# Three attention layers in one kernel: Q and K as two float32r halves instead of three bf16 parts, heads in pairs

## The chip, the cores and the metric

One core of one Trainium2 chip runs the whole program in one launch. The metric is the device time in microseconds; each run reports the time of its one core. TensorE (PE) multiplies matrices into PSUM, VectorE (DVE), ScalarE (ACT) and GpSimd (POOL) work on tiles, and SyncE (SP) issues the DMAs. All engines have queues of their own that run in order and are tied together by semaphores.

## The reference, cut to what matters

The input x is 2048 tokens by 256 features, float32. Eight residual blocks follow each other: attention A, a gated feed-forward block, a linear attention with a running sum, the feed-forward block again, attention B, a "hyperbolic" projection, attention C, the projection again. Each starts with a layer norm. All three attentions have 16 heads of 16 features:

```python
# A: causal by multiplication: masked scores are 0 and still count in the softmax
scores = einsum('bthd,bshd->bhts', q, k) * tril
out = softmax(scores / T ** 0.5) @ v
# B: not causal, the difference of two attentions with 8 features a head
score = softmax(attn1 - lam * attn2)        # done as one product over 16 features
# C: causal, one rotary term shared by all heads
scores = (einsum('bhtd,bhsd->bhts', q, k) + einsum('btd,bsd->bts', qr, kr)[:, None]) / sqrt(16 + 64)
```

The weights are scaled so that scores are large. The kernel takes care that they come close to float32 products, and subtracts the true row maximum before the exponential.

## The kernel before, in words

**Parts.** After a projection, VectorE rounds a 128 x 512 tile of Q or K to bf16 (L1165) and takes the remainder (L1166); ScalarE rounds the remainder to bf16 (`middle_part`, L1052), GpSimd takes what is left (`split`, L652), and SyncE writes the three parts to DRAM (`parts_to_dram`, L450). The staging tile `STG` has two buffers; VectorE waits for the DMA of the tile two before. `load_stacks` (L479) reads the parts back as stacks: 16 rows for each of six part products (0·0, 0·1, 0·2, 1·0, 1·1, 2·0), so a head's score is one bf16 matmul over 96 rows. `KROWS` is 99: three more rows carry minus the row maximum in three bf16 parts on the Q side, against rows of ones on the K side. Each group of four heads has its own stack, 12 DMAs of 256 KB, double-buffered by group. The first group's stack comes in four token chunks.

**Two passes.** Scores are computed twice. The first pass has the queries on partitions (`max_piece`, L868), 512 keys a piece, one head after the other; VectorE reduces each bank to a row maximum (L1304; on the diagonal, L1300, with the mask, and in layer C, L1293, with the rope scores added, each by a multiply-and-reduce that waits for the previous one). Per chunk of 512 queries, `neg` (L1315 to L1320) combines the maxima and splits their negative into three bf16 parts, four waits between five operations; TensorE transposes them (`mtr`, L894), VectorE copies the result (L1326), four small DMAs put it into the Q stack (L498). The second pass has the keys on partitions (L916): a unit is one key block of 128 against a chunk of 512 queries, with one score matmul a head, ScalarE's exponential (L1079), and `pv` (L940), four heads on the four 32-column tiles, float32. A unit's `pv` stands two units behind (`LAG`), in the queue ahead of the last two scores of the current unit. Layer A has extra units "e" and "m" for the zero scores beyond the diagonal. In layer C 24 of the 40 units add the rope product on TensorE (`rope_product`, L744, three bf16 matmuls a head); 16 get stored rope scores added by VectorE (L1311).

**Rings and order.** PSUM banks 0 to 3 are four slots for maxima and transposes, 4 to 6 a ring of three for scores, 7 holds the `pv` sum. A score waits for the exponential three scores before it. `Layer.plan` writes the order of steps by hand-set weights: the maxima of the next group (and of later chunks) are spread between the score and `pv` steps of this one, in proportion to their weights. All engines walk the same list. A first list (`L.first`) holds maxima only, the last (`L.last`) has none for a next group. SyncE walks the list too: it issues the maximum rows' DMAs and, in C, the loads of rope scores into a ring of five (L502), after the next group's stack loads.

The ring's wait, as it stands now:

```python
n = L.exp_no[u] + j
if n >= RING2:                                   # RING2 = 3
    pe.wait_ge(L.exp_done, group * L.n_exp + (n - RING2 + 1))
```

## Time and profile before

| | us |
|---|---|
| median of 3 runs (lowest, highest) | 3143.9 (3142.0, 3153.44) |
| span of the profiled execution | 3148.2 |
| TensorE busy | 2717.8 (86%) |
| VectorE busy | 2173.0 (69%) |
| ScalarE busy | 1342.8 (43%) |
| GpSimd busy | 312.2 (10%) |

The page gives no other time for the profiled execution than its span, which runs from the first to the last instruction; so the span is its own time here. The page's clock row stands at 9 or 8 tenths in most slices and at 5 to 8 where a layer begins. Layer A's main stage lies at 153 to 718 us, B's at 1267 to 2048, C's at 2345 to 3071; before each there is a stage of maxima only and a stage of projections, and between A and B the feed-forward and linear blocks (750 to 1150 us). Busy time is what an engine's instructions cover; a matmul's duration is modelled and longer than the distance between starts, so starts are what to read on TensorE.

### The profile page before, as it was taken

What the parts mean: (1) busy time and instruction counts of PE and PEld (TensorE: products, weight loads), DVE (VectorE), ACT (ScalarE), POOL (GpSimd) and SP (SyncE); (2) the same over time, 40 slices, a digit from 0 to 9 for tenths busy, and PEclk for the clock granted to TensorE, in tenths of its full rate; (3) what the DMA queues carried; (4) which work ended last, traced back from release to release, by engine and by line L of the source; (5) the groups of instructions that cost most, each with busy time, mean ns of one, the idle gap of its engine ahead of it and who ended that gap; (6) DMA issues with size and microseconds to landing.
All of it is one profiled execution on the core that took longest, in us unless ns stands there. A gap on an engine that the chain in (4) does not pass through costs nothing. (4 is left out here: it accounts for less than half of the span.)

```text
span 3148.2 us, 44751 instructions
## 1 busy us (share of the span) xinstructions
PE 2717.8 (86%) x14184; PEld 1063.8 (34%) x14184; DVE 2173.0 (69%) x5325; ACT 1342.8 (43%) x2654; POOL 312.2 (10%) x764
## 2 busy tenths in 40 slices
PE   6688889899999996999999999967759878798995
PEld 4122323225565552222222222243213333333334
DVE  6667667644445446888888888386568868687857
ACT  2055556572111110566666666712104434344451
POOL 4122221210000011000000000002100010100110
PEclk9599889999999996999999999987859999899998
DMA  5502130000000016003003000003651151411100
GB/s 167 95 2 31 13 42 2 2 1 17 1 1 1 14 35 125 1 1 41 1 1 42 1 2 1 1 14 121 212 95 46 51 90 45 84 50 50 52 30 27
DMA packets 90291, 126.58 MB, mean 40 GB/s; under 512 B 14128, under 2 KB 63536, under 8 KB 89904
## 3 DMA queue, kind: packets, MB, share of 16 engines
q1 hardware_dynamic: 90032, 123.54, 18.1%
q8 instruction: 112, 1.84, 0.3%
q14 instruction: 147, 1.20, 0.1%
HBM read 89.36 MB, written 33.55 MB: 39 GB/s over the span
## 5 line engine op out<-in xcount | busy, mean ns | idle before, releaser
L1079 ACT ACTIVATE PF<-PS 128x512 f32<-128x512 f32 (+3 forms) x2368 | 1185.5, 567 | 1076.7 <-PE PS L916 596.9
L1304 DVE TENSOR_REDUCE MP<-PS 128x1 f32<-128x512 f32 x1408 | 888.2, 684 | 173.0 <-PE PS L868 171.5
L868 PE MATMUL PS<-KF,QF 96*128 96x512 bf16 (+3 forms) x2304 | 837.5, 392 | 76.7 <-DVE MP L1293 32.1
L916 PE MATMUL PS<-QF,KF 99*128 99x512 bf16 (+3 forms) x2304 | 763.1, 375 | 99.7 <-ACT PF L1079 87.3
L940 PE MATMUL PS<-PF,VG 128*32 128x512 f32 (+3 forms) x5120 | 611.0, 558 | 9.9 <-POOL PF L672 9.7
L868 PEld LDWEIGHTS PS<-KF,QF 96*128 96x128 bf16 x2304 | 215.9, 99 | 647.1 <-DVE MP L1304 291.2
L916 PEld LDWEIGHTS PS<-QF,KF 99*128 99x128 bf16 x2304 | 223.1, 99 | 505.2 <-ACT PF L1079 371.3
L744 PE MATMUL PS<-WA 128*128 128x512 bf16 (+3 forms) x1320 | 291.0, 338 | 12.1 <-DVE HT L1231 12.0
L672 POOL TENSOR_SCALAR_AFFINE_SELECT PF<-PF 128x128 f32<-128x128 f32 x512 | 144.5, 292 | 1170.5 <-ACT PF L1079 1153.8
L739 PE MATMUL PS<-HT,WA 128*128 128x512 f32 x512 | 221.1, 592 | 0.0
L1293 DVE CUSTOM_DVE_ANT_0 JUNK<-PS,WC 128x512 bf16<-128x512 f32 (+3 forms) x256 | 159.5, 623 | 80.1 <-PE PS L868 28.8
L1293 DVE CUSTOM_DVE_ANT_0 JUNK<-PS,WA 128x512 bf16<-128x512 f32 (+3 forms) x256 | 151.3, 591 | 68.6 <-DMA WA<-rope_scores 24.3
L940 PEld LDWEIGHTS PS<-PF,VG 128*32 128x32 f32 x5120 | 108.3, 111 | 238.2 <-ACT PF L1079 137.4
L1300 DVE CUSTOM_DVE_ANT_0 JUNK<-PS,MASKS 128x128 bf16<-128x128 f32 (+3 forms) x256 | 125.8, 492 | 69.1 <-PE PS L868 36.0
L744 PEld LDWEIGHTS PS<-WA 128*128 128x128 bf16 x1320 | 125.4, 100 | 125.7 <-issue 17.0
L739 PEld LDWEIGHTS PS<-HT,WA 128*128 128x128 f32 x512 | 96.6, 190 | 118.6 <-issue 115.7
L993 ACT COPY HT<-PS 128x512 f32<-128x512 f32 x64 | 34.5, 588 | 226.7 <-PE PS L773 226.7
L1137 DVE TENSOR_TENSOR X<-PS,X 128x512 f32<-128x512 f32 x48 | 33.1, 690 | 134.0 <-PE PS L841 99.5
L652 POOL TENSOR_TENSOR PF<-PF 128x512 bf16<-128x512 f32 (+1 forms) x56 | 64.6, 1154 | 543.8 <-ACT PF L1052 543.8
L1329 DVE COPY OS<-PS 128x512 f32<-128x512 f32 x48 | 33.1, 689 | 118.7 <-PE PS L940 117.9
L841 PE MATMUL PS<-WA,QF 128*128 128x256 f32 x512 | 111.8, 379 | 0.0
L1036 ACT ACTIVATE PF<-PS 128x512 f32<-128x512 f32 x64 | 38.2, 597 | 167.5 <-PE PS L739 167.5
(130 smaller groups left out, 1892.7 us busy)
## 6 DMA issues: line engine op xcount, KB each, us to landing
WC<-rope_scores SPq DMA_DIRECT2D x48, 256.0 KB, 3.1
WA<-rope_scores SPq DMA_DIRECT2D x40, 256.0 KB, 3.1
rope_scores<-HT SPq DMA_DIRECT2D x28, 256.0 KB, 2.4
MASKS<-rope_scores SPq DMA_DIRECT2D x24, 256.0 KB, 3.1
QF<-parts_a_q SPq DMA_DIRECT2D x18, 256.0 KB, 12.3
KF<-parts_a_k SPq DMA_DIRECT2D x18, 256.0 KB, 13.8
QF<-parts_b_q SPq DMA_DIRECT2D x18, 256.0 KB, 12.6
KF<-parts_b_k SPq DMA_DIRECT2D x18, 256.0 KB, 14.3
```

The lines of the kernel that those rows point to most:

```text
L652: g_.tensor_tensor(STG[0:rows, n % 2, 2, :], TA[0:rows, n % 2, :], STG[0:rows, n % 2, 1, :], ALU.subtract)\
L672: g_.affine_select(out=tile, in_=tile, compare_op=ALU.is_ge, fill=0.0, base=0, pattern=[[1, P]], channel_multiplier=-1).then_inc(L.mask_do ...
L739: ins = mm(dst, left(k), right(k), start=k == 0, stop=k == n - 1)
L744: ins = mm(dst, RS[:, left[r], l0:l0 + m], RS[:, right[r], r0:r0 + n], start=start and r == 0, stop=r == 2)
L841: ins = mm(bank(b, D, i * D), GT[:, m, blk(2 * h + i)], WDT[:, m, :], start=m == 0, stop=m == HID // P - 1)
L868: ins = mm(bank(slot + x, width), QS[0:SROWS, off + j * T + tb * P:off + j * T + (tb + 1) * P], KS[0:SROWS, off + j * T + s0:off + j * T + ...
L916: ins = mm(dst, k, q, start=True, stop=not rope)
L940: ins = mm(PS[32 * j:32 * j + 2 * DH, 7 * CH + t0:7 * CH + t1], V, PT[:, u % SETS, j, t0:t1], start=first, stop=last, tile_position=(0, 32 ...
L1079: sc.activation(PT[:, u % SETS, j, off:CH], bank(4 + n % RING2, CH - off), ACT.Exp).then_inc(L.exp_done, 1)
L1293: ins = v.tensor_tensor_reduce(out=JUNK[:, 0:w], in0=src, in1=AR[a % AR_RING][:, 0:w], scale=1.0, scalar=LOWEST, op0=ALU.add, op1=ALU.max, ...
L1300: ins = v.tensor_tensor_reduce(out=JUNK[:, 0:w], in0=src, in1=MASKS[:, 0 if L.zeros else 1, MW - w:MW], scale=1.0, scalar=low, op0=ALU.mul ...
L1304: ins = v.reduce_max(dst, src, AX.X)
```

## The change

Q and K are split into two parts, float32r for the first and the float32 remainder for the second, both made by VectorE alone; ScalarE's and GpSimd's steps are gone. Of the part products three are kept: 0·0, 0·1, 1·0. A head takes 48 rows plus 2 for the maximum. Two heads lie one above the other, at rows 0 and 64, and their matmuls run on the two 64-row tiles of the array, into two different banks. Bytes of a stack stay the same: 12 DMAs of 256 KB (16 rows x 2 pairs x 2048 x 4 bytes). Maxima and scores go by pairs of heads: a step is a pair, with two slots of two banks for the maxima and the same ring of three banks for scores. The plain maximum is one reduction over 2 x 512; the masked and the rope ones stay two instructions with one wait for the pair. The rope product takes two float32r matmuls instead of three bf16. The ones rows of the key stack come by DMA, and the negated maximum has two parts.

```diff
-PARTS = 3
-SROWS = 6 * DH
+PARTS = 2
+PRODUCTS = ((0, 0), (0, 1), (1, 0))
+PAIRS = HG // 2
+HALF = P // 2
+SROWS = len(PRODUCTS) * DH
...
-            for x in range(0, w, CH):
-                ones.append((min(CH, w - x) / CH + (0.2 if x + CH >= w else 0), ("max", n, x // CH)))
+            ones.append((2 * w / CH + 0.2, ("max", n)))
...
-                r = 4 if self.rope else 1
-                if u in self.added:
-                    r = 0.2
-                twos += [(r * width(u), ("score", u, j)) for j in range(HG)]
+                cost = 6 if self.rope and u not in self.added else 1.5
+                twos += [(cost * width(u), ("score", u, r)) for r in range(PAIRS)]
...
-                at = len(twos) - 2 if twos[-1][1][:2] == ("score", u) else len(twos)
+                at = len(twos) - 1 if twos[-1][1][:2] == ("score", u) else len(twos)
...
+            def one_rows():
+
+                for h in range(2):
+                    dst = KS[HALF * h + MROW:HALF * h + KROWS, :].bitcast(F32).rearrange("i (n t) -> i n t", t=P)
+                    src = ONE[0:PARTS, :].unsqueeze(1).to_broadcast([PARTS, 2 * PAIRS * NB, P])
+                    sp.dma_start(dst, src).then_inc(ones_in, 16)
...
                 for n in pieces:
-                    for dst, w, i in ((QS, "q", (0, 0, 0, 1, 1, 2)[n]), (KS, "k", (0, 1, 2, 0, 1, 0)[n])):
-                        x = dst[n * DH:(n + 1) * DH, bass.ds(parity * (HG * T), HG * T)]
-                        sp.dma_start(x.rearrange("d (j t) -> d j t", j=HG)[:, :, t], rows(w, i)).then_inc(L.stack_in, 16)
+                    product, h = n // 2, n % 2
+                    for dst, w, i in ((QS, "q", PRODUCTS[product][0]), (KS, "k", PRODUCTS[product][1])):
+                        row = HALF * h + product * DH
+                        x = dst[row:row + DH, bass.ds(parity * (PAIRS * T), PAIRS * T)]
+                        sp.dma_start(x.bitcast(F32).rearrange("d (r t) -> d r t", r=PAIRS)[:, :, t], rows(w, i, h)).then_inc(L.stack_in, 16)
...
+            sp.wait_ge(const_ready, N_CONST)
+            one_rows()
             for kind, steps in PROGRAM:
...
-            constant(g_.memset(KS[MROW:KROWS, :], 1.0))
...
             def rope_product(dst, left, l0, m, right, r0, n, start=True):
-                for r in range(3):
+                for r in range(PARTS):
...
+            def max_pair(L, n, slot, off):
+
+                r, tb, i, s0, w, diag = L.jobs[n]
+                o = off + r * T
+                for h in range(2):
+                    rows = slice(HALF * h, HALF * h + SROWS)
+                    ins = mm(bank(slot + h, w), QS[rows, o + tb * P:o + (tb + 1) * P], KS[rows, o + s0:o + s0 + w], start=True, stop=True)
+                ins.then_inc(L.slot_ready, 1)
...
-                        if n >= RING2:
-                            pe.wait_ge(L.exp_done, group * L.n_exp + (n - RING2 + 1))
+                        n = L.exp_no[u] + 2 * r
+                        if n + 1 >= RING2:
+                            pe.wait_ge(L.exp_done, group * L.n_exp + (n - RING2 + 2))
+                        rope = L.rope and u not in L.added
+                        for h in range(2):
+                            rows = slice(HALF * h, HALF * h + KROWS)
+                            k = ONESEL[rows, :] if kind == "e" else KS[rows, o + sb_ * P:o + (sb_ + 1) * P]
+                            ins = mm(bank(4 + (n + h) % RING2, CH - off), k, QS[rows, o + c * CH + off:o + (c + 1) * CH], start=True, stop=not rope)
+                            if not rope:
+                                ins.then_inc(L.score_ready, 1)
+                        if rope:
+                            for h in range(2):
+                                rope_product(bank(4 + (n + h) % RING2, CH - off), ROPE_K, sb_ * P, P, ROPE_Q, c * CH + off, CH - off,
+                                             start=False).then_inc(L.score_ready, 1)
...
-                        link(v.tensor_scalar(STG[:, n % 2, 0, :], bank(b), factor, None, ALU.mult))
-                        v.scalar_tensor_tensor(out=TA[:, n % 2, :], in0=bank(b), scalar=factor, in1=STG[:, n % 2, 0, :],
+                        link(v.tensor_scalar(STG[:, n % 2, 0, :].bitcast(F32R), bank(b), factor, None, ALU.mult))
+                        v.scalar_tensor_tensor(out=STG[:, n % 2, 1, :], in0=bank(b), scalar=factor, in1=STG[:, n % 2, 0, :],
                                                op0=ALU.mult, op1=ALU.subtract).then_inc(d_free, 1)
...
+                        src = PS[:, slot * CH:(slot + 2) * CH].rearrange("p (h s) -> p h s", h=2)[:, :, 0:w]
+                        dst = MP[:, i, tb // BPC, 2 * r:2 * r + 2, tb % BPC]
                         if L.rope:
 
                             if n > 1:
                                 dve.wait_ge(L.slot_free, n - 1)
...
+                            for h in range(2):
+                                ins = v.tensor_tensor_reduce(out=JUNK[:, h * CH:h * CH + w], in0=src[:, h], in1=AR[a % AR_RING][:, 0:w], scale=1.0,
+                                                             scalar=LOWEST, op0=ALU.add, op1=ALU.max, accum_out=dst[:, h:h + 1])
...
-                        clink(v.tensor_scalar(NM[:, :, 0], MX[:, 0], -1.0, None, ALU.mult))
-                        clink(v.scalar_tensor_tensor(out=MX[:, 1], in0=MX[:, 0], scalar=-1.0, in1=NM[:, :, 0],
-                                                     op0=ALU.mult, op1=ALU.subtract))
-                        clink(v.tensor_copy(NM[:, :, 1], MX[:, 1]))
-                        v.tensor_tensor(NM[:, :, 2], MX[:, 1], NM[:, :, 1], ALU.subtract).then_inc(L.neg_ready, 1)
+                        clink(v.tensor_scalar(NM[:, :, 0].bitcast(F32R), MX[:, 0], -1.0, None, ALU.mult))
+                        v.scalar_tensor_tensor(out=NM[:, :, 1], in0=MX[:, 0], scalar=-1.0, in1=NM[:, :, 0],
+                                               op0=ALU.mult, op1=ALU.subtract).then_inc(L.neg_ready, 1)
```

## Rows read from the trace of the kernel before

**Rows 1.** The page's busy times: us, share, instructions; granted clock in 40 slices.
```profile
PE 2717.8 (86%) x14184; PEld 1063.8 (34%) x14184; DVE 2173.0 (69%) x5325; ACT 1342.8 (43%) x2654; POOL 312.2 (10%) x764
...
PEclk9599889999999996999999999987859999899998
```

**Rows 2.** Busy us (instructions) by stretch: PE, PEld, DVE, ACT, POOL; clock, DMA share, GB/s.
```profile
153.00:718.00 565.00, 495.68 (x3643) 164.39 (x3642) 365.94 (x908) 326.50 (x704) 140.62 (x392) 0.92 0.10 13
1267.00:1997.00 730.00, 704.13 (x3838) 192.97 (x3837) 628.59 (x1077) 487.12 (x944) 4.29 (x12) 1.00 0.08 10
1997.00:2048.00 51.00, 44.83 (x261) 9.97 (x259) 3.90 (x12) 41.48 (x81) 0.00 (x0) 1.00 0.00 1
2345.00:3010.00 665.00, 576.19 (x3349) 221.06 (x3348) 516.85 (x1488) 292.80 (x566) 70.52 (x242) 0.93 0.26 58
```

**Rows 3.** Timeline of one unit of layer B: start us, us, engine, line, work, idle before.
```profile
1606.46 0.39 PE L868 MATMUL PS<-KF,QF 96*128 96x512 bf16 x1
...
1606.89 2.48 DVE L1304 TENSOR_REDUCE MP<-PS 128x1 f32<-128x512 f32 x4 [0.63 <-PE PS L868]
...
1607.11 2.06 ACT L1079 ACTIVATE PF<-PS 128x512 f32<-128x512 f32 x4 [0.77 <-PE PS L916]
...
1608.00 0.38 PE L868 MATMUL PS<-KF,QF 96*128 96x512 bf16 x1
...
1608.31 1.06 PE L940 MATMUL PS<-PF,VG 128*32 128x512 f32 x8
...
1609.31 0.39 PE L868 MATMUL PS<-KF,QF 96*128 96x512 bf16 x1
```

**Rows 4.** Timeline of layer B's last stretch, scores and values only.
```profile
2010.45 0.39 PE L916 MATMUL PS<-QF,KF 99*128 99x512 bf16 x1 [0.26 <-ACT PF L1079]
...
2010.77 1.07 PE L940 MATMUL PS<-PF,VG 128*32 128x512 f32 x8
...
2011.77 0.82 PE L916 MATMUL PS<-QF,KF 99*128 99x512 bf16 x3
...
2012.19 2.07 ACT L1079 ACTIVATE PF<-PS 128x512 f32<-128x512 f32 x4 [0.33 <-PE PS L916]
...
2012.85 0.39 PE L916 MATMUL PS<-QF,KF 99*128 99x512 bf16 x1 [0.26 <-ACT PF L1079]
```

**Rows 5.** Timeline of layer C, VectorE.
```profile
2707.57 0.69 DVE L1293 CUSTOM_DVE_ANT_0 JUNK<-PS,WA 128x512 bf16<-128x512 f32 x1
...
2708.19 0.08 DVE L1293 DVE_READ_ACCUMULATOR2_ANT MP<- 128x1 f32 x1
...
2708.41 0.69 DVE L1293 CUSTOM_DVE_ANT_0 JUNK<-PS,WA 128x512 bf16<-128x512 f32 x1
```

**Rows 6.** Waits in one group of layer C: us in total, times, longest.
```profile
DVE JUNK L1293 <- DMA WC<-rope_scores: 13.0, 1, 13.0
```

**Rows 7.** Timeline of layer B's projection, first steps of two tile pairs.
```profile
1176.38 0.69 DVE L1165 TENSOR_SCALAR PF<-PS 128x512 bf16<-128x512 f32 x1 [3.59 <-DMA parts_b_q<-PF]
...
1177.83 0.62 ACT L1052 CAST PF<-PF 128x512 bf16<-128x512 f32 x1 [4.39 <-DVE PF L1166]
...
1178.53 1.15 POOL L652 TENSOR_TENSOR PF<-PF 128x512 bf16<-128x512 f32 x1 [3.86 <-ACT PF L1052]
...
1182.73 0.75 DVE L1165 TENSOR_SCALAR PF<-PS,QSC 128x512 bf16<-128x512 f32 x1 [2.82 <-DMA parts_b_k<-PF]
```

**Rows 8.** The page's DMA issues: count, KB each, median us to landing.
```profile
residual<-X SPq DMA_DIRECT2D x4, 512.0 KB, 3.2
```

**Rows 9.** Timeline of a negation chain of layer B.
```profile
1602.96 0.17 DVE L1317 SCALAR_TENSOR_TENSOR MX<-MX,NM 128x16 f32<-128x16 f32 x1
...
1603.70 0.22 PE L894 MATMUL PS<-IDB,NM 128*48 128x128 bf16 x1 [1.27 <-DVE NM L1320]
```

**Rows 10.** Groups by form, float32: busy us, mean ns, then idle before.
```profile
L739 PE MATMUL PS<-HT,WA 128*128 128x512 f32 x512 | 221.1, 592 | 0.0
L739 PEld LDWEIGHTS PS<-HT,WA 128*128 128x128 f32 x512 | 96.6, 190 | 118.6 <-issue 115.7 <-DVE PF L1192 2.8
```

More of the change, by code:

```diff
@@ L24 @@
 F32 = mybir.dt.float32
+F32R = mybir.dt.float32r
 BF16 = mybir.dt.bfloat16
@@ L108, in __init__ @@
         self.plan()
-        ring = lambda steps: sum(s[0] in ("mtr", "otr") or (s[0] == "max" and s[2] == 0) for s in steps)
+        ring = lambda steps: sum(s[0] in ("mtr", "otr", "max") for s in steps)
         self.r_first, self.r_stage = ring(self.first), ring(self.stage)
@@ L171, in plan @@
             n_lead += 1
-        while (ones[n_lead][1][0] == "max" and ones[n_lead][1][2] > 0) or ones[n_lead][1][0] == "mtr":
+        while ones[n_lead][1][0] == "mtr":
             n_lead += 1
@@ L639, in _ @@
             constant(g_.tensor_scalar(MASKS[:, 1, :], MASKS[:, 0, :], -1.0, -LOWEST, ALU.add, ALU.mult))
-            link(g_.memset(ONESEL[:], 0.0))
-            constant(g_.memset(ONESEL[MROW:KROWS, :], 1.0))
+            link(g_.memset(ONESEL[:].bitcast(F32), 0.0))
+            rows = [HALF * h + MROW + i for h in range(2) for i in range(PARTS)]
+            for row in rows:
+                ins = g_.affine_select(out=ONESEL[:], in_=ONESEL[:].bitcast(F32), compare_op=ALU.not_equal, fill=1.0, base=-row,
+                                       pattern=[[0, P]], channel_multiplier=1)
+                if row == rows[-1]:
+                    constant(ins)
+                else:
+                    link(ins)
             constant(g_.memset(ONE[:], 1.0))
@@ L1045, in main @@
                     sc.activation(NW[:, 5, :], NW[:, 4, :], ACT.Tanh).then_inc(n2_tanh, 1)
-            parts, rope_parts = Count(), Count()
-            def middle_part(rows, ready, count):
-                n = parts.next() - 1
-                act.wait_ge(ready, count)
-                sc.copy(STG[0:rows, n % 2, 1, :], TA[0:rows, n % 2, :]).then_inc(middle_ready, 1)
             def norm_copies(c):
```

273 lines of the change are left out of this document (117 added, 156 removed).

## The prediction

> **What bounds the kernel now.** The page's busy shares come first [rows 1]: TensorE 86%, VectorE 69%. That is a mean over stages, so the busy time by stage comes next [rows 2]: in layer B's main stage TensorE is busy 704 of 730 us at full clock, in layer A's 496 of 565, in layer C's 576 of 665 with VectorE at 517 beside it. The three take 1960 of the 3148 us.
>
> Then the timeline, one unit of layer B (one key block, four heads) [rows 3]. Eight matmuls (four maximum products, four scores) start 0.22 us apart, 1606.46 to 1608.00 in seven steps; the value product (pv, eight instructions on four column tiles) starts 0.31 us after the last and the next matmul 1.00 us after that. 1606.46 to 1609.31 is 2.84 us, and TensorE starts something new all the way: B is bound by the number of TensorE instructions. VectorE needs 2.48 us for its four reductions (0.60 apart), ScalarE 2.06 us for four exponentials.
>
> In B's last 51 us no maxima are left [rows 2, 4]. TensorE would need 4 x 0.22 + 1.3 = 2.2 us a unit, yet a unit takes 2.40 (2010.45 to 2012.85). That is the ring of three PSUM banks: score to exponential 0.42 (2011.77 to 2012.19), exponential 0.59, semaphore 0.06, score; and pv stands in the queue between scores.
>
> In C VectorE binds. Each maximum with rope scores waits on the one before: starts 0.84 apart, 0.69 busy plus the accumulator read, then 0.14 idle [rows 5]. A group has 160 of them, narrower ones included. The main stage holds some 580, so 80 us of such gaps stand beside the 517 busy [rows 2]. Once a group it also waits 13 us for rope scores queued behind the 3 MB of the next group's stacks [rows 6].
>
> **The change part by part.**
>
> *Split in two parts.* Today a tile goes VectorE, ScalarE (0.62), GpSimd (1.15), DMA; with two staging buffers, two tiles take 1176.38 to 1182.73 = 6.35, other cycles 6.5 [rows 7]. The two middle steps go: 1.8 us per two tiles. The tile's DMA grows from 384 to 512 KB; a 512 KB transfer lands in 3.2 us [rows 8] against about 3.0 between GpSimd's end and VectorE's next start. What is late next is that DMA. B: 8 x 1.8 = 14. A 11 (its first chunk waits on TensorE). C has 24 tiles but also waits for other work: 9. The last tile's path before the stacks, in A and B: 4. Sum -38. The stack loads keep number and bytes, so C's 13 us stalls stay. SyncE's new wait for constants and its two ones-row DMAs lie before any tile is ready: nothing; uncovered, some 3 us. The constants that used to fill the key rows go, hidden as well.
>
> *Row maxima chain.* Two of five linked operations of the negation go. Three of them and the semaphore to TensorE take 1602.96 to 1603.70 = 0.74, so some 0.21 each; TensorE waits in order for the transpose behind them (1.27 idle) [rows 9]. 48 x 0.41 = 20; I take -16, as some are covered. The float32 transpose and the maximum rows' DMA (4 for 3 KB) I take as unchanged.
>
> *Maxima in pairs, B.* One reduction of 1024 for two of 512: 0.60 apart is 512 elements plus 0.07, so about 1.13 for 1.20. VectorE's floor is then 2.27 a unit. Nothing on the path of the main stage, 38 pairs x 0.07 = -3 in B's opening.
>
> *Matmuls in pairs, B.* The trace has no float32r and no row tiles. Nearest rows: bf16 at 0.22 per 512 columns, and four column tiles of pv, whose eight float32 instructions together take 1.0 [rows 3]; so tiles do run beside each other. A float32 matmul of two passes takes 221.1 / 512 = 0.43 a pass [rows 10]. Per pair the bounds are 0.22 (bf16 rate, side by side) and 0.43 (a pass's rate, or the heads one after the other). Half the moving data per pair at bf16's rate is the design's premise and bf16 is the row nearest in shape; I take 0.22 plus 0.03 for the second weight load. TensorE's load falls from 2.84 to about 2.0 a unit. That doesn't give 2.0, because the ring takes over. A pair needs two of three banks, so it waits for the first exponential of the pair before. A unit in queue order is score pair, maximum, pv, maximum, score pair (pv goes ahead of the last score step as before; the planner's weights, 1.5, 4.3, 1.5 against 2.2 for a maximum pair, put one on either side of pv in 0.8 of the units each). Chain: score to pv 0.32, pv 1.00, score to exponential 0.42, exponential 0.59, semaphore 0.06: 2.39, the 2.40 of the tail [rows 4]; plus 1.6 maximum pairs x 0.22 = 2.74. Against 2.84 that gives 0.10 x 236 units = -24. The tail's 20 units gain nothing.
>
> *A.* 28 wide units a group behave as in B, 112 x 0.10 = -11; the 16 narrow ones have short exponentials, where a ring by pairs is worse than by heads, but A's VectorE drops the wait inside a pair on the diagonal. I take -16 in all, ends -50 and +30.
>
> *C.* The second reduction of a pair no longer waits: 80 x 4 x 0.14 = 45, on the engine that binds. I take -32, since added rope scores now come by pairs and couple VectorE and ScalarE. Three rope matmuls a head become two, on an engine that has room then.
>
> *Costs that no row shows.* Second weight load: 2.6 intervals a unit x 0.03 in A and B, +30 (ends 0 and +100 with a float32 load's 0.19 [rows 10]). Changing between 64-row tiles and the full array for rope: 96 units x 4 changes; maximum to pv starts 0.31 against 0.22, so 0.09 a change [rows 3], 35 if on the path. C is VectorE's: I take +10.
> The Trainium skill ("TensorEngine Tiling (Array Packing)", Key Properties) says that changing the tiling mode, not just the tile, drains TensorE; by that rule the 35 would fall due wherever TensorE binds, and the sum would be 25 worse.
>
> Sum: -38 - 16 - 3 - 24 - 16 - 32 + 30 + 10 = -89. The profiled execution's span is 3148, 4 above the median 3144: 3055 as a median. I round to 3050.
>
> **Rivals.**
> *Float32r streams at a float32 pass's rate*, 0.43 per 512 columns on full array and tiles alike [rows 10]. For: the only 4-byte matmuls in the trace do so. Against: they are two-pass products, and float32r needs one. B's unit: 2.39 + 0.21 (score to pv) + 1.6 x 0.43 + 0.21 (score to exponential) = 3.50, 0.66 x 236 = +156; A about +94; C's rope two at 0.43 instead of three at 0.22, +40. With the gains outside (-89): 3349, so 3345.
> *Slower by the pair's interval*: the two weight loads come one after the other at 0.19, or the two heads overlap only in part, so a pair takes 0.38. Every pair between two scores lengthens the chain: 2.39 + 0.16 + 1.6 x 0.38 = 3.16, +76 in B, +49 in A, +20 in C, less the 89: 3200. It decides from about 0.35 a pair; below that the gains outside attention win. For it: 0.19 in the float32 rows. Against: pv's eight loads and matmuls, on column tiles, fit into 1.0 [rows 4].
> The Trainium skill ("TensorE: Matmul & The Clock Gate", LDWEIGHTS) gives a load's time as its columns over 1.2 GHz whatever the rows, an estimate of 0.11 for 128 columns and 0.21 for two in a row; by it a pair would just stay at 0.22.
> *The ring doesn't bind* and VectorE's 2.27 plus chunk ends does: B 2.35 a unit, another -70 to -95, A another -30: about 2930. For: ScalarE has slack now. Against: the tail's 2.40 without any maximum.
> *Clock*: a TensorE 70% busy might be granted less. Against: B's tail shows 45 of 51 busy at 1.00; the page's clock falls to 6 tenths only where B begins, with maxima alone [rows 1]. It stretches the upper side only.
>
> **How the numbers follow.** Forecast 0.54, float32 rate 0.12, pair interval 0.14, ring free 0.14, clock or other 0.06. Within 0.5% (about what a measurement tells from no change) is 3128 to 3160. Faster: 0.46 of the forecast and all of ring free, 0.61, and some of the pair's case below break-even: 0.65. Slower: 0.12 + 0.08 + 0.04 = 0.24; same 0.11. Range 2940 (ring nearly free) to 3230 (past the pair case); the float32 rate is left out above. The likeliest case alone: 3000 to 3110.
>
> **What would show it.** Pairs start 0.22 to 0.26 after each other in B's unit; units 2.7 to 2.9; ScalarE waits once a unit for the score pair behind pv; TensorE's busy share in B well under 96%; one 1024-wide reduction of about 1.2; projection cycles of about 4.7; C's second reduction 0.70 after the first. B units near 3.2 or 3.5, or a matmul start interval over 0.35, would make it wrong to the slow side; units of 2.35 to the fast side.

## The result, and the profile after

The changed kernel takes 3353.8 us (median of four, 3311.8 to 3375.2) against 3148.0 beside it on the same chip: ratio 1.056, 95% interval 1.052 to 1.061. The forecast was 3050, range 2940 to 3230. It is slower, and outside the range. The ratio is that of its two shorter executions (3311.8 and 3336.1), while the trace read below is of a longer one (span 3369.5, granted clock 0.830, against 3310.1 at 0.852 in the shortest), so that its stages show rather too much of the loss.

The page of the changed kernel, lines as in [rows 1]:

```profile
PE 2678.3 (79%) x13744; PEld 1187.8 (35%) x13744; DVE 2068.8 (61%) x4525; ACT 1342.9 (40%) x2598; POOL 237.0 (7%) x709
...
PEclk9558969869999987999879998687677877877778
```

VectorE's work fell by 104 us and GpSimd's by 75, as they should; TensorE issues 440 fewer matmuls. The clock row has 7, 6 and 5 where the one of before has 9. By stretch, columns as in [rows 2], for A, B, B's tail and C:

```profile
140.00:757.00 617.00, 498.71 (x3616) 190.93 (x3616) 336.55 (x696) 337.18 (x696) 140.97 (x385) 0.78 0.09 12
1309.00:2110.00 801.00, 646.90 (x3929) 206.97 (x3925) 597.36 (x575) 526.43 (x970) 4.28 (x12) 0.92 0.07 9
2110.00:2158.00 48.00, 40.46 (x150) 9.32 (x150) 0.00 (x0) 24.96 (x46) 0.00 (x0) 0.50 0.00 1
2452.00:3200.00 748.00, 602.55 (x2971) 269.86 (x2971) 486.32 (x1440) 281.86 (x562) 68.47 (x237) 0.79 0.24 51
```

In A, B and C TensorE is busy 81% where it was 88, 96 and 87, and no other engine is over 75%: what binds is not one busy engine but a loop of waits between them. And the clock is 0.78, 0.92 and 0.79 where it was 0.92, 1.00 and 0.93; B's tail, the stretch from which the forecast argued that an emptier TensorE keeps its clock, runs at half clock throughout.

A unit of B at full clock (timeline, columns as in [rows 3]):

```profile
1400.90 0.50 PE L874 MATMUL PS<-KFR,QFR 48*128 48x512 f32 x2
1401.00 0.19 PEld L917 LDWEIGHTS PS<-QFR,KFR 50*128 50x128 f32 x2
1401.24 0.40 PE L917 MATMUL PS<-QFR,KFR 50*128 50x512 f32 x2
1401.44 1.23 DVE L1295 TENSOR_REDUCE MP<-PS 128x2 f32<-128x1024 f32 x1 [0.20 <-PE PS L874]
1401.67 1.09 ACT L1070 ACTIVATE PF<-PS 128x512 f32<-128x512 f32 x2 [0.74 <-PE PS L917]
1402.38 0.22 PEld L917 LDWEIGHTS PS<-QFR,KFR 50*128 50x128 f32 x2 [1.19 <-issue]
1402.41 0.50 PE L917 MATMUL PS<-QFR,KFR 50*128 50x512 f32 x2 [0.78 <-ACT PF L1070]
...
1402.72 0.43 PE L874 MATMUL PS<-KFR,QFR 48*128 48x512 f32 x2
1403.00 1.08 ACT L1070 ACTIVATE PF<-PS 128x512 f32<-128x512 f32 x2 [0.24 <-PE PS L917]
...
1403.08 1.07 PE L944 MATMUL PS<-PF,VG 128*32 128x512 f32 x8
...
1404.08 0.50 PE L874 MATMUL PS<-KFR,QFR 48*128 48x512 f32 x2
```

The order is the forecast's: maximum pair, score pair, wait, score pair, maximum pair, pv. Its length is 3.18: 0.34 to the score pair, 0.43 to its exponential, 0.59 for that, 0.12 until the next score pair's weights load, 0.34 to the maximum pair, 0.36 to pv, 1.00 for pv. And behind the wait the load is bare: from it to the exponential is 0.62, not 0.42 [rows 4].

Now every unit, from the first instruction of its pv to that of the next, set beside the same unit of the kernel before (same position in the stage), and sorted by the clock that it got in the changed kernel:

| stage | full clock: units, mean after (before) | half clock | partly at half clock |
|---|---|---|---|
| A | 113: 2.65 (2.72) | 63: 3.80 (2.82) | 15: 5.15 (4.94) |
| B | 209: 3.07 (3.06) | 35: 4.19 (2.54) | 11: 5.36 (4.03) |
| C | 64: 3.50 (3.50) | 18: 7.42 (5.50) | 77: 6.09 (5.07) |

B's median unit at full clock is longer, 3.09 against 2.84, but the old kernel has more units of 3.0 and 3.3 between them, so the means are the same. So at full clock all three stages run as fast as before, and the time lost lies in units that are wholly or partly at half clock: 58 + 15 of B's 76 us, 113 of C's 113, and in A 65, of which the others give 8 back. The wait in each unit doesn't bring the clock down by itself: 209 of B's 255 units keep it. B's longer half-clock stretches begin with the long unit from one group to the next (8.8 to 9.5 us; 7.4 before, when the clock held), behind a unit of 4.0 at a chunk's end, and in the tail.

The waits of TensorE in B's stage (us, times, longest); the same view of before has none for a PF:

```profile
PE PS L917 <- ACT PF L1070: 139.1, 246, 0.8
PE PS L898 <- DVE NM L1309: 12.7, 15, 0.8
```

Once a unit TensorE stands 0.56 us for an exponential. In A that wait grew from 8.8 us to 88.6, in C from 73.6 to 138.4.

The small steps. Negation chain, C's reductions, and two steps of B's projection:

```profile
1391.63 0.17 DVE L1308 TENSOR_SCALAR NM<-MX 128x16 fp32r<-128x16 f32 x1
...
1392.16 0.27 PE L898 MATMUL PS<-IDF,NM 128*32 128x128 f32 x1 [0.85 <-DVE NM L1309]
```

```profile
2471.85 0.68 DVE L1283 CUSTOM_DVE_ANT_0 JUNK<-PS,MASKS 128x512 bf16<-128x512 f32 x1
...
2472.46 0.69 DVE L1283 CUSTOM_DVE_ANT_0 JUNK<-PS,MASKS 128x512 bf16<-128x512 f32 x1
```

```profile
1202.44 0.69 DVE L1156 TENSOR_SCALAR PF<-PS 128x512 fp32r<-128x512 f32 x1 [1.48 <-DMA parts_b_q<-PF]
...
1207.28 0.74 DVE L1156 TENSOR_SCALAR PF<-PS,QSC 128x512 fp32r<-128x512 f32 x1
```

The chain is short (0.85 idle for 1.27 [rows 9]); the second reduction of a pair in C starts 0.61 after the first, against 0.84 [rows 5]; two tiles take 1202.44 to 1207.28 = 4.8, forecast 4.7, before 6.35 [rows 7]. That is one of the short ones: over B's sixteen tiles two take 5.45 on average, before 6.47.

And one step that the forecast put at nothing, at the very start, first before and then after:

```profile
6.41 13.75 POOL L645 MEMSET KF<- 3x16384 bf16 x1
6.64 13.55 DVE L1124 TENSOR_SCALAR NW<-MV 128x4 f32<-128x4 f32 x1
```

```profile
6.38 0.95 POOL L660 MEMSET VG<- 128x1024 f32 x1
...
6.72 0.63 DVE L1115 TENSOR_SCALAR NW<-MV 128x4 f32<-128x4 f32 x1
```

The fill of the key stack's rows of ones is gone. In both kernels VectorE's small instruction ends with the GpSimd memset that runs beside it, so it took 13.55 us before and takes 0.63 now, and the first projected tile is reached at 22.0 instead of 34.8 us.

Where the 221 us between the two profiled spans are (a stage runs from its first pv to its last; the clock is that of the same stretch; "rest" is all else). The kernels of the experiments stand in the same table; its times are medians of all executions, while A, B, C and rest add up to the span of the one profiled.

| kernel | time (ratio, interval) | A | B | C | rest | clock A, B, C |
|---|---|---|---|---|---|---|
| before | 3148 | 560 | 772 | 714 | 1102 | 0.92 1.00 0.94 |
| after | 3354 (1.056, 1.052-1.061) | 617 | 849 | 826 | 1078 | 0.78 0.89 0.79 |
| e_fill | 3295 (1.047, 1.042-1.052) | 574 | 814 | 827 | 1077 | 0.93 1.00 0.85 |
| e_order | 3323 (1.055, 1.050-1.060) | 615 | 761 | 877 | 1069 | 0.77 0.92 0.77 |
| e_wide (on before) | 3190 (1.014, 1.010-1.018) | 558 | 818 | 707 | 1106 | 0.93 0.97 0.94 |
| e_split | 3482 (3397 to 3543, too far apart for a ratio) | 643 | 934 | 814 | 1065 | 0.71 0.77 0.79 |
| e_slots | 3346 (1.062, 1.056-1.068) | 574 | 868 | 823 | 1072 | 0.86 0.87 0.79 |
| e_full | 3409 (1.084, 1.080-1.087) | 617 | 909 | 795 | 1087 | 0.95 1.00 0.90 |
| e_bfill (on before) | 3285 (1.045, 1.042-1.048) | 627 | 774 | 771 | 1105 | 0.97 1.00 0.98 |
| e_mix | 3750 (1.190, 1.187-1.193) | 645 | 1202 | 832 | 1076 | 0.92 0.80 0.78 |
| e_mix2 | 3378 (1.069, 1.061-1.076) | 655 | 743 | 898 | 1087 | 0.88 0.95 0.82 |
| **e_ring4** | **3086 (0.981, 0.979-0.983)** | 492 | 757 | 728 | 1099 | 0.94 0.98 0.84 |
| e_ring4o | 3205 (1.019, 1.016-1.022) | 493 | 883 | 723 | 1094 | 0.92 0.90 0.87 |
| **e_bring4 (on before)** | **3076 (0.977, 0.975-0.979)** | 535 | 741 | 692 | 1110 | 0.92 1.00 0.96 |
| e_cfill | 3128 (0.994, 0.990-0.998) | 493 | 778 | 757 | 1099 | 0.93 0.94 0.92 |
| e_cfill2 | 3185 (1.012, 1.006-1.017) | 494 | 772 | 811 | 1099 | 0.93 0.95 0.97 |

So A +57, B +77, C +112, everything outside the three stages -24. (The clock of a stretch gives its time at half clock: 2 x (1 - clock) x length. For the whole span that is 497 us before and 1146 after.)

### The profile page after: what moved, and what is told of

It reads as the page before. It is cut to its first block and busy times, and to the rows that moved or that the text cites. A ratio compares the mean times of both kernels' runs of the same rounds, so it can differ in the third digit from the quotient of the medians.

```text
span 3369.5 us, 42504 instructions
## 1 busy us (share of the span) xinstructions
PE 2678.3 (79%) x13744; PEld 1187.8 (35%) x13744; DVE 2068.8 (61%) x4525; ACT 1342.9 (40%) x2598; POOL 237.0 (7%) x709
## 5 line engine op out<-in xcount | busy, mean ns | idle before, releaser
L1295 DVE TENSOR_REDUCE MP<-PS 128x2 f32<-128x1024 f32 x704 | 847.6, 1223 | 314.7 <-PE PS L874 313.6
L917 PE MATMUL PS<-QFR,KFR 50*128 50x512 f32 (+3 forms) x2304 | 597.4, 515 | 375.6 <-ACT PF L1070 374.8
L944 PE MATMUL PS<-PF,VG 128*32 128x512 f32 (+3 forms) x5120 | 714.1, 644 | 1.1 <-POOL PF L681 1.1
L874 PE MATMUL PS<-KFR,QFR 48*128 48x512 f32 (+3 forms) x2304 | 580.2, 506 | 117.1 <-DVE MP L1283 51.1
L917 PEld LDWEIGHTS PS<-QFR,KFR 50*128 50x128 f32 x2304 | 248.4, 212 | 812.9 <-ACT PF L1070 734.9
L874 PEld LDWEIGHTS PS<-KFR,QFR 48*128 48x128 f32 x2304 | 252.8, 218 | 557.3 <-issue 236.8
L747 PE MATMUL PS<-WAR 128*128 128x512 f32 (+3 forms) x880 | 266.3, 435 | 18.1 <-DVE HT L1222 16.3
L1283 DVE CUSTOM_DVE_ANT_0 JUNK<-PS,MASKS 128x512 bf16<-128x512 f32 (+2 forms) x256 | 157.7, 653 | 83.4 <-PE PS L874 64.6
L747 PEld LDWEIGHTS PS<-WAR 128*128 128x128 f32 x880 | 167.0, 224 | 97.1 <-issue 52.9
L1303 DVE TENSOR_TENSOR PS<-PS,X 128x512 f32<-128x512 f32 x128 | 82.9, 693 | 57.6 <-PE PS L917 57.4
```

Of the source, the lines that this page charges most:

```text
L747: ins = mm(dst, RS[:, left[r], l0:l0 + m], RS[:, right[r], r0:r0 + n], start=start and r == 0, stop=r == PARTS - 1)
L874: ins = mm(bank(slot + h, w), QS[rows, o + tb * P:o + (tb + 1) * P], KS[rows, o + s0:o + s0 + w], start=True, stop=True)
L917: ins = mm(bank(4 + (n + h) % RING2, CH - off), k, QS[rows, o + c * CH + off:o + (c + 1) * CH], start=True, stop=not rope)
L944: ins = mm(PS[32 * j:32 * j + 2 * DH, 7 * CH + t0:7 * CH + t1], V, PT[:, u % SETS, j, t0:t1], start=first, stop=last, tile_position=(0, 32 ...
L1283: ins = v.tensor_tensor_reduce(out=JUNK[:, h * CH:h * CH + w], in0=src[:, h], in1=AR[a % AR_RING][:, 0:w], scale=1.0, scalar=LOWEST, op0=A ...
L1295: ins = v.reduce_max(dst, src, AX.X)
```

## The experiments

**m_rates: what the instructions cost.** Stretches of one kind of matmul back to back.

> A kernel of matmul sequences alone (the output is a copy of x; attention and all else are left out): 64 at a time, each with weights of its own, after bf16 matmuls that bring the clock up. Theory 1 (float32r streams at bf16's rate, the pair is held up by its weight loads): 96-row bf16 0.216 us a matmul, 128-row float32r 0.22, a 48-row float32r pair 0.31 to 0.34 as in the changed kernel's layer B, the same pair in bf16 0.22. Theory 2 (float32r at a float32 pass's rate): 128-row float32r 0.43, pair 0.43. Theory 3 (the two row tiles do not overlap): the pair 0.43 in bf16 too. A change between pair and 128-row matmuls costs 0.09 by the prediction's row; between pair and pv as between a full matmul and pv.

Windows (TensorE's busy us and count first; the clock is the first number behind the brackets) inside the stretches of bf16 96-row, float32r 128-row, float32r 48-row all on one tile (two windows), float32r 48-row in pairs, bf16 48-row in pairs; then pairs alternating with pv:

```profile
26.00:39.00 13.00, 13.00 (x62) 5.89 (x61) 0.00 (x0) 0.00 (x0) 1.00 0.00 1
45.00:58.00 13.00, 13.00 (x59) 10.74 (x58) 0.00 (x0) 0.00 (x0) 1.00 0.00 1
64.40:68.70 4.30, 4.30 (x19) 3.50 (x20) 0.00 (x0) 0.00 (x0) 1.00 0.00 0
69.00:85.00 16.00, 16.00 (x39) 12.21 (x39) 0.00 (x0) 0.00 (x0) 0.50 0.00 0
96.00:110.00 14.00, 14.00 (x126) 13.02 (x124) 0.00 (x0) 0.00 (x0) 1.00 0.00 1
116.00:129.00 13.00, 13.00 (x124) 5.84 (x120) 0.00 (x0) 0.00 (x0) 1.00 0.01 1
```

```profile
202.95 0.49 PE L58 MATMUL PS<-WR 48*128 48x512 f32 x2
...
203.38 1.06 PE L71 MATMUL PS<-WF 128*32 128x512 f32 x8
...
204.37 0.49 PE L58 MATMUL PS<-WR 48*128 48x512 f32 x2
```

62 counts in 13 us are 0.21 each for bf16; float32r takes 0.22 to 0.23; 126 in 14 us are 0.22 a pair. So neither rival holds in that form: float32r runs at bf16's rate and two heads overlap fully. The 0.31 to 0.34 that I expected for a pair back to back was wrong as well. What a pair costs shows only where the kind of matmul changes: pair to pv 0.43 (bf16 to pv 0.32), and a sequence of a pair and two 128-row products, 24 times in 26.15 us, takes 1.09 instead of 0.23 + 0.46, so 0.20 a change, with the load that is bare behind it counted in. And one row tile alone, without a gap, ran at 0.23 a product at first (19 in 4.3 us) and then at half clock, 0.41 (39 in 16); pairs kept full clock.

**e_fill: the clock.** Ahead of a unit's first score pair, before the wait for its exponential:

```diff
+if r == 0 and kind == "s":       # wait for the next free slot, then, never read:
+    for _ in range(2):
+        for h in range(2):
+            mm(slot bank h, KS[rows, o:o + P], QS[rows, o:o + CH])
```

> The changed kernel with two more 48-row maximum pairs (their result is overwritten by the next slot's) ahead of each unit's first score pair, where TensorE stands idle: more work, same waits. If the lower clock is what makes the change slow, the half-clock time falls from 1135 us towards the 484 of before and the run gets faster than the changed kernel's 3312 to 3375, about 3200. If the longer chain at full clock is the cause, it stays the same or gets slower, by 0.65 us for each of 576 units where the gap is not there, up to +100.

2304 matmuls more and 77 us less between the two profiled executions; by the medians it is 59, and by the ratios 0.9%, with intervals that overlap a little (1.042 to 1.052, 1.052 to 1.061). The 3200 that I expected was far off. A is at 574 and B at 814 with the clock of before (0.93, 1.00); C has 0.85 and gains nothing. So in these two executions bringing the clock back is worth 43 us in A and 35 in B, with the fillers' own time already paid. A is still 14 and B 42 above before; part of that is the fillers' own time (B's full-clock units have a mean of 3.19 with them, 3.07 without).

**e_order and e_wide: the order and the slots.**

```diff
-while at < len(ahead) and given < (run + cost / 2) / whole * work:
+while at < len(ahead) and step[0] == "score" and step[2] == 0 and given < (run + cost / 2) / whole * work:
```

```diff
-L1 = Layer("b", False, False, False, CH, sem)
+L1 = Layer("b", False, False, False, 2 * CH, sem)
```

> The changed kernel with maxima handed out ahead of a unit's first score pair only, none on either side of pv. Chain theory: layer B's unit at full clock falls from 3.02 us by up to 1.6 x 0.33 to 2.5 to 2.7, total -100 to -170. Clock theory: TensorE's idle time gets shorter too, so some half-clock time goes as well. If VectorE's slots were the bound instead (two slots of pairs), the unit stays at 3.0 or grows, because both maxima come at once.

> The kernel before with one part of the change alone, in layer B: maxima by reductions of 1024, here two key pieces of one head, still bf16 and 96 rows. TensorE binds layer B before the change (2.84 us a unit), so the main stage stays the same; the opening gets 3 us shorter. If VectorE's 2.48 us had a share in the unit, B gets up to 20 us faster. Slower than before would say that coarser slots (two instead of four) cost by themselves.

With the maxima only ahead of the first score pair B takes 761, below before, and its full-clock unit 2.61, as the chain theory had it; C gets worse by 51 and A stays, so that the whole gains 31 by the medians and nothing by the ratio, not 100 to 170. Two slots of 1024 in place of four of 512 cost the kernel before 46 us in B (its median unit is 3.03, and its clock 0.97): coarser slots cost by themselves, against what I expected.

**e_split and e_slots: undoing the pair's wait, undoing its maximum.**

```diff
-if n + 1 >= RING2:
-    pe.wait_ge(L.exp_done, group * L.n_exp + (n - RING2 + 2))
 for h in range(2):
+    if n + h >= RING2:
+        pe.wait_ge(L.exp_done, group * L.n_exp + (n + h - RING2 + 1))
```

e_slots: `SLOTS = 4`, each head's bank waited for, reduced over 512 and freed by itself.

> The changed kernel, but each head of a score pair waits for its own PSUM bank: the first for the exponential three before, the second for the one after it (with the pair's single wait the first head waits for the second's bank). Theory 'the ring by pairs': a pair has only one exponential (0.59 us) of cover where single heads have two, and score to exponential is 0.62 in the changed kernel; then layer B's full-clock unit goes from 3.02 to about 2.85 and the time from 3354 to 3290-3310. Theory 'clock and mode changes alone': the pair's second head is what counts, both products start no earlier; unit 3.0, time within 15 of 3354.

> The changed kernel with the one maximum instruction a pair undone: products still in pairs on the two 64-row tiles, but each head has its own PSUM bank of a ring of four and its own 512-wide reduction, and frees its bank by itself. Theory 'coarse slots' (doubling the reduction in the kernel before cost 42 us, 46 in layer B): B loses 20 to 45 us of its 849, total 3300-3335. Theory 'clock and score ring': VectorE has spare time anyway and pays 0.07 more a pair: 3350-3375.

e_split is slower than the changed kernel: by 85 us between the shortest executions (3397 and 3312), by 128 between the medians; 3290 to 3310 was expected. At full clock it does what it should, a little: B's units have a mean of 3.02 (155 units) for 3.07. But its heads start apart, each alone on its tile:

```profile
1899.93 0.79 PE L917 MATMUL PS<-QFR,KFR 50*128 50x512 f32 x1 [0.26 <-ACT PF L1070]
...
1903.54 0.33 PEld L917 LDWEIGHTS PS<-QFR,KFR 50*128 50x128 f32 x1
...
1904.42 0.29 PEld L917 LDWEIGHTS PS<-QFR,KFR 50*128 50x128 f32 x1 [0.55 <-ACT PF L1070]
```

and the clock of B is 0.77. Its four executions order themselves by it: 3394.7 us at 0.809, 3455.6 at 0.788, 3503.9 at 0.771, 3541.1 at 0.759. In half-clock time (1297 to 1707 us) that is 0.36 us lost for each. The changed kernel's own four (3310.1 at 0.852 to 3373.4 at 0.825) give 0.31. This is a correlation: something that lengthens the waits may lower the clock as well. e_slots repairs A (574) and not B (868, where 20 to 45 less was expected) or C; over all its interval overlaps the changed kernel's.

**m_clock and m_clock2: which patterns keep the clock.** Units of 3.1 us, paced by exponentials, each ended by the value products where "pv" is said; each of the two kernels ran once.

> A kernel of its own (its output is a copy of an input, all else of the computation is left out): six stretches of 40 units, about 3 us a unit paced by five exponentials (2.7 to 3.0), each stretch after 150 bf16 matmuls back to back; a unit ends with the four value products. Matmuls ahead of them in a unit: (1) 4 float32r pairs on two 64-row tiles, 48 rows each; (2) 4 bf16 matmuls of 96 rows, about as long; (3) 8 such; (4) 4 float32r of 128 rows; (5) 8 pairs; (6) 1 pair. Theory 'tiles': the pairs' rows count, so stretch 1 is granted less than 2 and 4 at the same busy time, and 5 less than 3. Theory 'idle time': 1, 2 and 4 are granted the same, 3 and 5 full clock, 6 the least. Theory 'not the clock of such a pattern': all six at 1.0.

> As m_clock, again six stretches of 40 units of 3.1 us; in m_clock five patterns kept full clock (4 or 8 pairs, 96-row and 128-row matmuls, each with the value products) and only 1 pair with the value products lost it. Here: (1) 5 float32r products of 48 rows, all on the upper tile, and the value products; (2) 3 pairs and the values; (3) 8 pairs of 128 columns and the values; (4) 6 pairs without values; (5) 5 products of 48 rows without values, each behind one exponential, so apart; (6) the same and the values. Theory 'half-empty array': 1 and 6 lose the clock though TensorE has work most of the time, 2 and 4 keep it. Theory 'idle time alone': 1, 2, 4 and 6 keep it, 5 loses it.

Windows inside the stretches; m_clock 4 pairs + pv, 4 bf16 of 96 rows + pv, 1 pair + pv; then m_clock2 5 single 48-row + pv, 3 pairs + pv, 8 pairs of 128 columns + pv, 6 pairs, 5 singles apart (of the windows left out, three of m_clock have 1.00 and m_clock2's 5 singles apart with pv 0.50):

```profile
60.00:170.00 110.00, 78.06 (x572) 29.92 (x576) 0.00 (x0) 104.38 (x179) 0.00 (x0) 1.00 0.00 1
219.00:329.00 110.00, 72.90 (x432) 16.71 (x430) 0.00 (x0) 104.37 (x178) 0.00 (x0) 1.00 0.00 1
...
855.00:965.00 110.00, 94.81 (x360) 17.27 (x358) 0.00 (x0) 104.36 (x179) 0.00 (x0) 0.50 0.00 1
```

```profile
60.00:170.00 110.00, 110.00 (x337) 42.79 (x335) 0.00 (x0) 104.36 (x179) 0.00 (x0) 0.50 0.00 1
268.00:378.00 110.00, 70.29 (x504) 22.98 (x504) 0.00 (x0) 104.40 (x178) 0.00 (x0) 1.00 0.00 1
426.00:536.00 110.00, 110.00 (x704) 57.36 (x696) 0.00 (x0) 104.36 (x179) 0.00 (x0) 0.50 0.00 1
613.00:723.00 110.00, 104.28 (x430) 65.65 (x430) 0.00 (x0) 104.36 (x179) 0.00 (x0) 0.50 0.00 1
773.00:883.00 110.00, 58.99 (x180) 29.64 (x180) 0.00 (x0) 104.35 (x179) 0.00 (x0) 0.50 0.00 0
```

Both theories hold in part. Half-filled tiles cost the clock: five single-tile products and pv, which at full clock would take more of the unit (5 x 0.23 and 1.0, and changes) than 3 pairs do, lose it, as m_rates' single tile did without any gap, while 3 pairs and pv, busy 70 of 110 us, keep it. And idle time seems to cost it: 6 pairs in 3.1 us, or singles apart, lose it. Neither says why 8 pairs of 128 columns with pv do. Where exactly the changed kernel's own patterns fall between these wasn't measured pattern by pattern.

**e_full and e_bfill: a full array, and fillers for the kernel before.**

```diff
-rows = slice(HALF * h, HALF * h + SROWS)         # and + KROWS for scores
+rows = slice(0, HALF + SROWS)
```

> The changed kernel with no 64-row tile in attention: each head's float32r product takes rows 0 to 111 on the full array (both heads read the same rows, which adds their products; the rows between the halves are loaded with two small DMAs more a stack; the numbers computed are not the reference's, the instructions, bytes and order are). Same number of matmuls and loads, the same rings. Theory 'tiles': without mode changes and with more of the array busy the clock stays up; half-clock time falls from 1148 to below 700 us, layer C from 826 to 740-770, total 3200-3270, though a pair then takes 0.46 and not 0.23. Theory 'rings': the pair waits and the coarse slots remain and the product pairs are longer, so 3350-3420.

> The kernel before, with two 96-row bf16 filler products ahead of every other score step of layers A and C (results never read). It has 191 us at half clock in those two stages. Theory 'the clock is on the path there': A falls from 560 to about 535 and C from 714 to 690-700, total 3100-3130. Theory 'VectorE and the rings bind A and C, the clock falls because TensorE waits': fillers bring the clock up and no time, or cost their own 0.43 us: 3145-3200.

e_full brings the clock back (0.95, 1.00, 0.90) and is slower: its pairs start 0.46 apart and B's unit is 3.76. C alone gains 31. So the clock can be had by filling the array, but the time of the longer products is more than what it gives back (3409, where the theory of the tiles had 3200 to 3270 and the other 3350 to 3420). e_bfill raises the clock of A and C to 0.97 and 0.98 and costs 67 and 57 us, more than either theory had. So much of the fillers' time is on the path there; what the clock alone would be worth to the kernel before is not separated from it.

**e_mix and e_mix2: combinations.**

```diff
-cost = 6 if self.rope and u not in self.added else 1.5
+cost = 1.5 if not self.rope else 0.4 if u in self.added else 8
```

> The changed kernel with three edits of its schedule: two filler maximum pairs ahead of the first score pair of a unit in layers A and B (as in the filler kernel, not in C); in B maxima only ahead of that score pair (as in the order kernel, not in A and C); in C the planner's weights as in the kernel before, in proportion (8 instead of 6 for a rope score pair, 0.4 instead of 1.5 for one whose rope scores VectorE adds, and 2.2 for a maximum pair). By stage, if clock and queue order are the two causes in A and B: A 575 (e_fill), B 725 to 745 (the order kernel had 761 with 129 at half clock), rest 1075. C: 'weights' 760-790, so 3150-3185; 'weights do nothing' 826, 3200-3220.

> As e_mix, but the fillers stand in A and C, not in B. If the fillers' own time in B is small beside the clock that they hold: B 750 to 765 here against 725 to 745 there. C with the weights and fillers: 'fillers cost C what they give' the same as e_mix's C within 15; 'the clock is on C's path' 20 to 40 less.

Neither tests what it was made for: the fillers stand behind the wait for the exponential instead of ahead of it, so on the path (B 1202). What they still show: e_mix's C with the planner's weights and without fillers is 832 against 826, so the weights weren't C's loss; e_mix2's B, ordered and without fillers, is 743.

**e_ring4 and e_ring4o: the banks.** On e_slots:

```diff
-SLOTS = 4
+SLOTS = 3
-RING2 = 3
+RING2 = 4                       # scores in banks 3 to 6
+if slot + 1 >= SLOTS:           # a maximum pair waits for both its banks
+    pe.wait_ge(L.slot_free, slot + 2 - SLOTS)
```

> The changed kernel with the PSUM banks dealt out otherwise: the score ring has four banks (two whole pairs, so that a pair waits for the pair two before and has two exponentials of cover) and the maximum ring three single banks, with a 512-wide reduction for each head. Theory 'the ring by pairs costs the time': B's full-clock unit falls from 3.09 to 2.6-2.7, C's median from 4.1 to 3.7, TensorE is fuller and half-clock time falls below 900 us: 3200-3280. Theory 'clock and mode changes': unit about 3.0, 3320-3380.

> The same with B's maxima only ahead of a unit's first score pair (without ring4 that gave a B unit of 2.61 and a stage of 744 to 761). If the cover was missing only for want of order, B is 735-760 as there and A and C are e_ring4's; if both add, B is below 720.

One bank moved from the maxima to the scores takes 260 us off e_slots (3200 to 3280 was expected), and the result is 1.9% faster than the kernel before. B's stage in e_ring4, a 50 us window, its waits and a unit:

```profile
1201.00:1958.00 757.00, 630.33 (x4067) 212.44 (x4063) 634.31 (x1045) 526.91 (x1016) 4.29 (x12) 0.98 0.08 10
...
1500.00:1550.00 50.00, 41.33 (x275) 14.39 (x277) 45.40 (x75) 34.34 (x66) 0.00 (x0) 1.00 0.01 1
```

```profile
PE PS L876 <- DVE MP L1301: 96.5, 221, 0.6
...
PE PS L922 <- ACT PF L1075: 4.7, 15, 0.5
```

```profile
1500.47 0.50 PE L876 MATMUL PS<-KFR,QFR 48*128 48x512 f32 x2 [0.54 <-DVE MP L1301]
...
1501.89 0.50 PE L922 MATMUL PS<-QFR,KFR 50*128 50x512 f32 x2
...
1502.23 0.40 PE L876 MATMUL PS<-KFR,QFR 48*128 48x512 f32 x2
...
1502.47 0.40 PE L922 MATMUL PS<-QFR,KFR 50*128 50x512 f32 x2
```

The wait for the exponential is gone (139 us to 5). TensorE now waits for VectorE's reductions, 45.4 of 50 us busy, and a unit is 2.71 (mean 2.87, 245 units at full clock). A score pair right behind a maximum pair starts 0.24 after it; the first pair behind pv takes 0.34. In e_ring4o the bunched maxima meet a ring of three banks and B's unit is 3.18: there the order hurts where it helped with two slots of two banks.

**e_bring4: does the kernel before want that bank too?** The same three numbers changed in it (`RING2 = 4`, three slots, scores from bank 3).

> The kernel before with e_ring4's dealing of the banks: four for scores, three for maxima, all else as it was. By heads a score already has two exponentials (1.19 us) of cover and TensorE is busy 96% of B. Theory 'pairs need the fourth bank, heads don't': within 0.5% (3132 to 3164), B 772, A 560. Theory 'the fourth score bank is worth as much to either': A and B lose 40 or more each, below 3070, and the pairs have no part in e_ring4's 3086.

It does, against what I expected: -72 us, in A 25, B 31 and C 22. TensorE's waits in B's main stage did not show it beforehand (none for an exponential), and its median unit is 2.84 in both, but the mean is 2.90 against 3.03. Unit by unit, 8 of B's 31 us come from the tail, where a unit takes 1.97 (pv at 1975.19, next at 1977.16) against 2.40 [rows 4], and 23 from the main stage, where nearly half the units are about 0.2 us shorter. The prediction named the ring of three as what makes the tail 2.40, and took it as given for both kernels.

With the same banks the two kernels stand at 3086 and 3076, intervals touching: 10 us apart where it was 206. The change is worth nothing there or costs up to 0.8%, though e_ring4 has the shorter start of the changed kernel (13 us) and not its one reduction of 1024.

**e_cfill and e_cfill2: the clock once more,** on e_ring4, two 128-row fillers in C before the wait, once or twice a unit.

> e_ring4 with two filler products of 128 rows (rope operands, never read) in layer C ahead of a unit's first score pair, issued before TensorE waits for the exponentials. C in e_ring4 has 728 us, 243 of them at half clock. Theory 'the clock is on C's path' (0.3 us lost for each at half clock, from the spread of the executions of the changed kernel): half-clock time below 120, C 690-710, total 3050-3070. Theory 'C waits on its rings and the filler's 0.46 us a unit eats the gain': 3080-3130.

> The same with the two fillers ahead of both score pairs of a unit. 'Clock': C at full clock nearly throughout, 690-720 (the fillers' time counts twice), total 3050-3080. 'Rings': 3110-3180.

C's clock rises from 0.84 to 0.92 and 0.97 and C from 728 to 757 and 811, so the 690 to 720 of the clock theory are refuted. But the fillers take time themselves and first wait for a free slot; that the clock alone is worth nothing to C is not shown, only that it can't be had this way for less than it gives. In e_cfill and e_cfill2 B, where nothing was changed, was 15 to 21 us longer than in e_ring4 at a clock of 0.94 and 0.95, all of it in units at half clock or partly there; that spread is part of any comparison here.

## Why the prediction was wrong

Two steps failed. The larger is *Clock*: "Against: B's tail shows 45 of 51 busy at 1.00 ... It stretches the upper side only", with 0.06 for it and no time: the sum takes the clock as unchanged. The other, which called it up, is *Matmuls in pairs, B*: "2.39 ... plus 1.6 maximum pairs x 0.22 = 2.74".

- The clock. B's old tail had four products a unit on the full array and pv; the new one has two pairs and pv and runs at 0.50, and so do stretches of all three stages. The tail was the wrong row to argue from, and others spoke against it: in [rows 2] the stages with TensorE 88 and 87% busy, A and C, have 0.92 and 0.93, and the clock row of [rows 1] falls to 5 tenths where A and C begin, not "only where B begins". At full clock a unit takes what the same unit took before; all that the stages lose, but 4 us in B, lies in units wholly or partly at half clock. The fillers, which only add work, take off 43 and 35 in A and B. By the 0.31 us for each us at half clock, the shortest execution's 980 - 497 = 483 us more would be 150 of its 162, an upper estimate, as the slope also holds the waits that go with a lower clock.
- The chain. The ring did take over, as forecast, since a pair holds two of three banks. But the chain used 0.22 for a pair between others: in the trace it is 0.34 (0.36 before pv), because behind a wait or a change of tiling the float32r load, 0.18, isn't hidden, and 0.12 instead of 0.06 to the next load. So the median unit is 3.09 and not 2.74, and TensorE stands 0.56 us in each. "It decides from about 0.35 a pair" stood under the second rival, and 0.34 is nearly there, by the bare load and the change and not by the tiles: back to back a pair takes 0.22.
- A: -16 taken, +57 measured (ends -50 and +30). At full clock it gains 0.07 a unit (2.65 against 2.72); its 63 units at half clock lose 62 us.
- C: -32 taken on VectorE. The reductions did get closer (0.84 to 0.61, even more than thought), but TensorE's wait for exponentials rose by 65 and VectorE now waits 175 us for maxima instead of 49. C was counted on VectorE, which is 65% busy there now (78% before): it stopped being the bound.
- Projections: all outside the stages is 24 us shorter (forecast -38 and -3), but not as forecast. From the first tile to the last the projections of A, B and C are 7, 7 and 5 us shorter, forecast 11, 14 and 9; the 4 for the last tile's path didn't come; and 13 us come from the constants' fill, which the prediction called hidden. That the sum is not further off is luck. Negation chain: right in kind, TensorE's wait for it fell by 20, 5 and 3 us (forecast -16).
- Costs that no row showed: the second weight load, +30, and C's changes, +10. A change costs 0.20 (m_rates), not 0.09. The Trainium skill ("TensorEngine Tiling (Array Packing)", Key Properties) says that changing the tiling mode drains TensorE; m_rates agrees that it costs, and its 0.20 is the price here. The Trainium skill's time of a weight load ("TensorE: Matmul & The Clock Gate", LDWEIGHTS), by which the prediction estimates 0.11 for 128 columns, is near bf16's here (0.10); a float32r load takes 0.18.
- The rivals. Float32r at a float32 pass's rate: refuted. "The ring doesn't bind": e_ring4 is that case made real, and it gives 3086, not 2930: VectorE's four reductions of 512 (2.57 of a unit of 2.71) bind, and C keeps 728. In the two slower rivals A's +94 and +49 are more than its 112 units give by the same steps (74 and 36).

Shown: the score ring is what the pairs ran into. With three score banks the two kernels are 206 us apart, with four 10, and B's clock is back at 0.98; e_slots, which has e_ring4's separate reductions but not its fourth score bank, gains 8 us by the medians and nothing by the ratio. Where the time goes is shown too: in all three stages into units at half clock or partly there. Argued only: that the lost clock makes those units long, and not the other way round. For A and B the fillers speak for it (43 and 35 us back); for C nothing does, as fillers there raised the clock and brought nothing. The weights, the slots and the pair's wait are excluded as C's main loss (832, 823, 814 against 826); the fourth bank brings it to 728, against 692 for the kernel before with the same bank. Not tried: 1024-wide reductions with four score banks, for which a second slot of two banks has no room.

## What to carry to other kernels

When work is grouped, count what a group takes of each ring, and compare what is left as cover with the whole latency behind a wait, bare load included. Give a buffer to the ring whose wait stands on the path before changing the arithmetic: here that was worth 72 us to the old kernel without any other change. When a change makes TensorE wait, look up the nearest pattern in a trace with the same rows, tiles and gaps before assuming that it keeps its clock. Work added only to hold the clock paid once here (e_fill, some 59 us by the medians) and cost time in e_bfill, e_cfill and e_cfill2.

## What the hardware showed that was not expected

- Float32r, 512 columns: 0.22 to 0.23 us on 128 rows, and the same for two 48-row products side by side on the two 64-row tiles.
- The load of 128 float32r columns takes 0.18 (bf16 0.10); it hides back to back (64 products 0.23 apart) and not behind a wait.
- A change between 64-row tiles and the full array costs about 0.20 us; pair to pv 0.43 against bf16 to pv 0.32.
- One row tile alone, without a gap, falls to half clock; pairs without a gap don't. Value products and three pairs in 3.1 us hold full clock; six pairs without value products, eight pairs of 128 columns with them, or five products on single tiles with them, fall to half clock.
- A VectorE instruction on 128 x 4 elements begun beside a GpSimd memset ended with it, 13.55 us long before the change and 0.63 after.
